# Delta-rule layer: 32-row blocks swapped in every second tile with the solve in three stages, and the gate product as one rounded product over 96 rows

## The reference, cut to what matters

```
def delta_rule(q, k, v, beta):            # per sequence and per head, head size 32
    for each token t:
        pred  = k_t @ S                   # S is a 32x32 state
        delta = beta_t * (v_t - pred)
        S     = S + outer(k_t, delta)
        o_t   = q_t @ S

q = silu(x @ Wq.T); k = silu(x @ Wk.T); v = x @ Wv.T      # 16 heads of 32
beta = 2 * sigmoid(x @ Wbeta.T)
k = k * rsqrt(sum(k*k) + eps)
gate = sigmoid(x @ Wg1.T @ Wg2.T)         # Wg1 is 32x512, Wg2 512x32
og = delta_rule(q, k, v, beta) * gate
out = (og * rsqrt(mean(og*og) + eps)) * g_norm @ Wo.T
```

## Time and profile before

| | us |
|---|---|
| median of 3 runs | 4828.01 |
| lowest and highest | 4825.08, 4836.86 |
| the profiled execution's own time | 4826.68 |
| its span, first to last instruction | 4824.6 |
| PE busy (share) | 4466.7 (93%) |
| DVE busy | 3603.4 (75%) |
| ACT busy | 2416.7 (50%) |
| POOL busy | 707.2 (15%) |

### The profile page before, as it was taken

How to read it: one execution, slowest core, us unless ns; L and a number is a source line. 1 busy time by engine, 2 the same in 40 slices (tenths; PEclk the granted TensorE clock), 3 DMA queues, 4 the chain that set the end, 5 groups by cost and what they waited for, 6 DMA issues and landing times.

```text
span 4824.6 us, 144788 instructions
## 1 busy us (share of the span) xinstructions
PE 4466.7 (93%) x63104; PEld 3089.8 (64%) x63104; DVE 3603.4 (75%) x7890; ACT 2416.7 (50%) x4592; POOL 707.2 (15%) x909
## 2 busy tenths in 40 slices
PE   7999999999999985999999999999999999999998
PEld 6777777777887764565565565565565565565564
DVE  5777767777777773877877877877877877877876
ACT  3344444434444332646646646646646646645645
POOL 0000000000000001122122122122122122122121
PEclk8999999999999997999999999999999999999999
DMA  2223222222322222000000000000000000000000
GB/s 88 56 74 75 73 69 65 65 69 74 78 69 65 65 65 80 1 18 1 19 18 2 19 19 2 19 19 2 19 18 2 19 18 2 19 18 2 19 10 10
DMA packets 352135, 171.76 MB, mean 36 GB/s; under 512 B 300017, under 2 KB 300785, under 8 KB 350737
## 3 DMA queue, kind: packets, MB, share of 16 engines
q1 hardware_dynamic: 342528, 145.20, 11.3%
q10 hardware_dynamic: 8976, 17.30, 1.3%
HBM read 93.74 MB, written 67.63 MB: 33 GB/s over the span
## 4 chain that ended last, share of the span: by engine, by line
PE 45%; DVE 11%; ACT 2%; issue 1%; POOL 1%; DMA 1%; SPq 0%; DVEq 0%; ACTq 0%; POOLq 0%
PE row_psum L1720 10%; PE row_psum L1745 10%; PE row_psum L40 5%; PE row_psum L42 5%; PE row_psum L41 5%; DVE smax L2007 5%; PE row_psum L1733 4%; PE row_psum L1793 1%; DVE xr_lo L1868 1%; PE row_psum L1773 1%; DVE probs L1987 1%; PE row_psum L1507 1%; DVE stats L1834 1%; POOL rstd L1304 1%; PE row_psum L1692 1%
## 5 line engine op out<-in xcount | busy, mean ns | idle before, releaser
L2007 DVE TENSOR_REDUCE smax<-row_psum 128x1 f32<-128x512 f32 x2048 | 1270.5, 681 | 94.8 <-PE row_psum L1720 93.7
L1441 ACT ACTIVATE probs<-row_psum 128x512 f32<-128x512 f32 x2048 | 1090.7, 602 | 350.0 <-PE row_psum L1733 330.5
L1720 PE MATMUL row_psum<-k_stack,q_stack 64*128 64x512 f32 (+1 forms) x2048 | 740.5, 440 | 50.6 <-DVE smax L2007 24.4
L1733 PE MATMUL row_psum<-q_stack,k_stack 64*128 64x512 f32 (+1 forms) x2048 | 733.5, 458 | 20.3 <-ACT probs L1441 8.1
L1720 PEld LDWEIGHTS row_psum<-k_stack,q_stack 64*128 64x128 f32 (+1 forms) x2048 | 354.3, 188 | 499.3 <-DVE smax L2007 367.9
L1745 PE MATMUL row_psum<-probs,v_aug 128*32 128x512 f32 x4096 | 538.9, 603 | 1.7 <-ACT av_sb L1457 0.4
L1733 PEld LDWEIGHTS row_psum<-q_stack,k_stack 64*128 64x128 f32 (+1 forms) x2048 | 319.2, 184 | 223.3 <-ACT probs L1441 155.7
L894 DVE TENSOR_TENSOR lane_t<-lane_t,lane_p 128x30 f32<-128x30 f32 (+14 forms) x960 | 318.3, 332 | 33.0
L40 PE MATMUL row_psum<-wf_hi,xr_hi 128*128 128x320 f32 (+1 forms) x1024 | 332.0, 324 | 5.3 <-DVE xr_lo L1868 3.2
L891 DVE TENSOR_TENSOR lane_p<-lane_t 128x30 f32<-128x30 f32 (+14 forms) x960 | 316.0, 329 | 25.5
L42 PE MATMUL row_psum<-wf_hi,xr_lo 128*128 128x320 f32 (+1 forms) x1024 | 319.0, 312 | 0.0
(11 more groups left out here) (215 smaller groups left out, 9854.2 us busy)
## 6 DMA issues: line engine op xcount, KB each, us to landing
x_sp<-in_x ACTq DMA_DIRECT2D x33, 512.0 KB, 4.3
tri_dram<-tri SPq DMA_DIRECT2D x256, 64.0 KB, 3.2
lane_t<-tri_dram SPq DMA_DIRECT2D x32, 512.0 KB, 3.8
inv_dram<-lane_t SPq DMA_DIRECT2D x32, 512.0 KB, 2.7
inv_b<-inv_dram SPq DMA_DIRECT2D x256, 64.0 KB, 2.3
x_res<-in_x SPq DMA_DIRECT2D x32, 512.0 KB, 3.9
x<-x_res SPq DMA_DIRECT2D x32, 512.0 KB, 3.2
xs<-x SPq DMA_DIRECT2D x16, 1024.0 KB, 5.5
```

Of the source, the lines that this page charges most:

```text
L1441: act.activation(probs[:, h % PROBS, tt, :], ps[:, m % STACK_BANKS, :], ACT.Exp, scale=float(DH) ** -0.5).then_inc(exp_ready, 1)
L1720: pe.matmul(ps[:, bank, :], q_stack[rows, qt, P * st:P * st + P], k_stack[rows, kv, :], start=True, stop=True).then_inc(max_mm, 1)
L1733: pe.matmul(ps[:, m % STACK_BANKS, :], k_stack[rows, kv, P * tt:P * tt + P], q_stack[rows, qt, :], start=True, stop=True).then_inc(score_m ...
L2007: dve.tensor_reduce(smax[:, g, st:st + 1], ps[:, bank_of("max", NT * g + st), :], AX.X, ALU.max).then_inc(max_ready, 1)
```

## The change

**Blocks swapped.** In tile 1 of each span (and only there) the two 32-token blocks of every chunk change places. It is done where x is turned: the four transposes of tile 1 become matmuls with `ident_swapped`. All that follows from x (k, v, beta, the triangles) then has the swapped order in tile 1; `masks_swapped` fits the mask to it. q and gate are put back in token order where ACT takes them out of PSUM: one ACTIVATE for tile 0 and two for tile 1 in place of one for both. `upper` and `product` in tile 1 then read rows 32-63 and 96-127, and `under` reads 0-31 and 64-95.

**Three stages.** The solve becomes `solve_upper`, `solve_product`, `solve_under`, each with 64 matmuls, tile 0 and tile 1 in turn (`both_tiles`), and copies and corrections follow in the order 0, 2, 1, 3 of the groups.

**Gate product.** g1 becomes 96 rows of float32r: rounded, remainder, rounded; Wg2 the same rows as rounded, rounded, remainder. One float32r matmul over 96 rows replaces the float32 matmul over 32. ACT makes the third part (`take_gb`), DVE the second (`split_g1`, behind `correct_queries`).

**Loads at the start.** 4 small DMAs for `ident_swapped`, 12 for `masks_swapped`, 3 in place of 1 for Wg2, all on SP.

```diff
+        def blocks_of(ap, t, h):
+            if t == 0:
+                return ap[:, :, 0:P]
+            return ap[:, :, P:2 * P].rearrange("p g (c h r) -> p g c h r", c=2, h=2)[:, :, :, h, :]
+        def in_token_order():
+            return ((0, None), (0, None)), ((1, 0), (1, 1)), ((1, 1), (1, 0))
 ...
             def take_gb(b, s, first=False):
-                act.activation(g1, BB[0:HD, 0:SPAN], ACT.Copy).then_inc(g1_ready, 1)
+                act.activation(g1[0:HD, :], BB[0:HD, 0:SPAN], ACT.Copy).then_inc(g1_ready, 1)
 ...
+                act.wait_ge(g1_ready, at(b, s, 2, 1))
+                act.activation(g1[2 * HD:3 * HD, :], g1[0:HD, :].bitcast(F32), ACT.Copy).then_inc(g1_ready, 1)
             def take_q(b, s, n):
-                act.activation(kq[:, 2 * n:2 * n + 2, 1 + s, :], (BA, BC)[n][:, :].rearrange("p (g i) -> p g i", g=2),
-                               ACT.Silu).then_inc(q_ready, 1)
+                for place, tokens in in_token_order():
+                    last = act.activation(blocks_of(kq[:, 2 * n:2 * n + 2, 1 + s, :], *tokens),
+                                          blocks_of((BA, BC)[n][:, :].rearrange("p (g i) -> p g i", g=2), *place), ACT.Silu)
+                last.then_inc(q_ready, 1)
 ...
-                            last = pe.transpose((BA, BD)[n][:, SPAN * g + P * t:SPAN * g + P * t + P],
-                                                xn[:, t, P * k:P * k + P], ident[:, :])
+                            if t:
+                                last = pe.matmul(into, xn[:, t, P * k:P * k + P], ident_swapped[:, :], start=True, stop=True)
+                            else:
+                                last = pe.transpose(into, xn[:, t, P * k:P * k + P], ident[:, :])
 ...
+            def block(t, half, late):
+                first = 2 * NB * half + NB * (late if t == 0 else 1 - late)
+                return slice(first, first + NB)
 ...
-            def solve_first(b, s, ahead):
 ...
-                for q in range(2):
+                for n in range(2):
                     if ahead:
-                        pe.wait_ge(tri_ready, at(*ahead, TS * HPT, HPT + q + 1))
-                    for i in range(H):
-                        last = upper(b, s, q, i)
-                    last.then_inc(u0_mm, 1)
+                        pe.wait_ge(tri_ready, at(*ahead, TS * HPT, HPT + n + 3))
+                    both_tiles(upper, b, s, n, u0_mm)
+            def both_tiles(stage, b, s, n, done):
+                for i in range(H):
+                    last = [stage(b, s, 2 * t + n, i) for t in range(TS)]
+                for ins in last:
+                    ins.then_inc(done, 1)
+            def solve_product(b, s):
+                for n in range(2):
+                    pe.wait_ge(u0_ready, at(b, s, 2 * TS, 2 * n + 2))
+                    both_tiles(product, b, s, n, p_mm)
 ...
+            def split_g1(b, s):
+                dve.wait_ge(g1_ready, at(b, s, 2, 1))
+                dve.tensor_tensor(g1[HD:2 * HD, :], BB[0:HD, 0:SPAN], g1[0:HD, :].bitcast(F32), ALU.subtract).then_inc(g1_lo_ready, 1)
 ...
-                correct_lower(*now, 0, behind)
-                correct_lower(*now, 1, behind)
+                for q in IN_TURN:
+                    correct_lower(*now, q, behind)
                 invert_ahead("split")
                 invert_ahead("product")
-                correct_lower(*now, 2, behind)
-                correct_lower(*now, 3, behind)
```

More of the change, by code:

```diff
@@ L180, in _ @@
             sp.dma_start(ident[:, :], ident_in).then_inc(first_in, 16)
+            for pb in range(P // NB):
+                sp.dma_start(ident_swapped[NB * pb:NB * pb + NB, :],
+                             ident_in[NB * (pb ^ 1):NB * (pb ^ 1) + NB, :]).then_inc(first_in, 16)
             sp.dma_start(stage_gb, w_gb).then_inc(second_in, 16)
@@ L325, in take_gate @@
                     act.wait_ge(gate_proj, at(b, s, 2, n + 1))
-                    act.activation(gate[:, s, 2 * n:2 * n + 2, :], (BA, BB)[n][:, :], ACT.Tanh, scale=0.5).then_inc(gate_ready, 1)
+                    for place, tokens in in_token_order():
+                        last = act.activation(blocks_of(gate[:, s, 2 * n:2 * n + 2, :], *tokens),
+                                              blocks_of((BA, BB)[n][:, :].rearrange("p (g i) -> p g i", g=2), *place),
+                                              ACT.Tanh, scale=0.5)
+                    last.then_inc(gate_ready, 1)
             def k_inverse_norms(b, s):
@@ L422, in step @@
                     turned(*further)
-                take_upper(*now, 0)
-                take_upper(*now, 1)
+                for q in IN_TURN:
+                    take_upper(*now, q)
                 if further:
                     take_k(*further, 0)
-                take_upper(*now, 2)
-                take_upper(*now, 3)
-                if further:
                     take_k(*further, 1)
-                for q in range(2 * TS):
+                for q in IN_TURN:
                     take_lower(*now, q)
@@ L578, in upper @@
                 h, half = 8 * n + i // 2, i % 2
-                r = slice(2 * NB * half, 2 * NB * half + NB)
+                r = block(t, half, 0)
                 return pe.matmul(bank[4 + q][r, 2 * HD * (h % 8):2 * HD * (h % 8) + 2 * HD],
@@ L586, in product @@
                 h, half = 8 * n + i // 2, i % 2
[L587 to L589 removed]
+                r = block(t, half, 0)
+                return pe.matmul(bank[4 + q][block(t, half, 1), 2 * HD * (h % 8):2 * HD * (h % 8) + 2 * HD],
+                                 tri[r, s, t, h // HPT, h % HPT, NB * (1 - t):NB * (1 - t) + NB], uw[r, t, h, :], start=True, stop=True)
             def under(b, s, q, i):
@@ L975, in begin @@
                 split_x(*second)
+                split_g1(*second)
                 statistics(*third)
@@ L1005, in step @@
                 correct_queries(*now)
+                if further:
+                    split_g1(*further)
                 invert_ahead("queries")
```

112 lines of the change are left out of this document (58 added, 54 removed).

## The result

The changed kernel takes 4784.6 us (median of 4 runs, 4783.4 to 4800.5), the kernel before 4831.6 us beside it (4 runs, 4825.1 to 4836.9): ratio 0.9913, 95% interval 0.9899 to 0.9927. The forecast was 4789, inside 4762 to 4824. The profiled execution took 4785.5 us with a span of 4783.7.

What follows compares the result with a forecast made beforehand. PE's work was taken as the bound, instruction supply just above its use. Per step -1.35 (solve) -1.24 (gate) +0.49 (ACT) +0.80 (supply) = -1.30 us, over 30 steps -39 us: 4789 us, range 4762 to 4824.

Steps and rivals of the forecast that it cites:

- What bounds the kernel: Whole step: a sum of PE work, PE busy 93% of the span, with instruction supply of 74 per us just above consumption.
- Stages, -1.90 us: Solve: three stages instead of four, each taken as 1.90 us, saving 1.90 us a step.
- The rival with 3.6 us a stage: New solve stages: tiles writing one PSUM bank don't run together, +3.0 us a step, 4917 us; chance 0.05.
- The later first `project_k`, +0.55: Start of the solve: first stage waits for the third triangle's banks, so the first key projection starts 0.55 us later.
- The gate product, -1.24, and +0.65 given back: Chains: two gate products save 0.62 us each; waits for instructions take back 0.65 us a step.
- ACT's pieces, +0.49: Behind the last chain: gate ACTIVATEs split in three per bank add 0.49 us a step on the path, bounds 0 to 1.3.
- DVE's slack, 1.3 us: DVE's gapless stretch after the lanes arrive: 22.5 us, ending 1.3 us before the first state advance is due.
- the DVE rival: DVE's inversion becomes the bound once PE no longer waits for instructions: 4777 us; chance 0.08.
- A wait of L704 for the state: In the chains: PE waiting for DVE's state was named as a sign that the forecast is wrong.
- The start, 0 within -2 and +5: Kernel start: 18 more DMAs on SP, delay nearly covered by room before Wv is needed; 0 us, between -2 and +5.
- The last two steps, 0: Last two steps, without gate or projections: the chain of copies stays as long as before, 0 us.
- nothing given back: Instruction supply takes nothing back, structure alone: -2.10 us in each of 30 steps, 4765 us; chance 0.22.

Runs made afterwards that it cites:

- e5: Changed kernel with the transitions' 128 tiny MATMULs issued twice in every step; some 140 us slower than the changed kernel (145 by medians, 136 by ratios).
- e9: Changed kernel with five extra 512-column float32r MATMULs inside the chains, ahead of the first gate product; 4796.4 us beside 4781.6.
- e2: Kernel before with the rounded 96-row gate product alone, solve and pieces as before; 19 us faster than the kernel before.
- e1: Changed kernel with the gate product put back to four float32 MATMULs of 24 rows; 28 us faster than the kernel before.
- e4: Changed kernel with the gate's tanh in one ACTIVATE per bank, not three pieces; step 54.66 us, gain not shown in the times.
- e10: The changed kernel itself run once more beside later runs on the same chip; 4781.6 us, ratio 0.9900.
- e8: Kernel before with DVE's last two corrections ahead of the inversion in the step without a further span; 3.5 us faster, interval 0 to 10.

## Why the prediction came out right, step by step

- **What bounds the kernel.** Right: PE's own work, with the supply of its instructions close to it. The packets' records, e5 and e9 show the supply; e2 shows what it takes from a gain. The prediction calls 74 per us the most that the queue brings; it was the mean of a stretch in which PE used 69. The shortest distances between packets give 75 to 80, so the number was near, by luck in part.
- **Stages, -1.90 us.** Right: -1.93 in the stretch, 1.92 us a stage. The rival with 3.6 us a stage is out (its own terms sum to +3.4 us a step, not the +3.0 written there, which changes nothing). What the Trainium skill states (TensorEngine Tiling (Array Packing), "Gotcha 1: PSUM Pressure") would have made these stages long. Here two row groups of one tile write one bank, and 128 MATMULs on four row groups take the 1.92 us that 64 on two took before (1.90).
- **The later first `project_k`, +0.55.** The mechanism is right (L953, 17.7 us in 30 steps), the size was low: +0.72 in a step like that of the rows (3.29 to 4.01), +0.90 on the mean. 0.17 us of it I left out: L908's third start is 1.24 us behind the first, and I added 0.62 for its end where the rows of after have the upper start 2.03 us behind the first triangle, not 1.86. The rest are waits for instructions ahead of the uppers and `project_k`, where I had put 0.15 for the whole solve; e1 shows 0.35.
- **The gate product, -1.24, and +0.65 given back.** Right as a sum: -0.56 in the chains against -0.59. e2 gives -0.57 there and +0.7 us of issue waits; the timed runs of e2 are 19 us below before, and with the 4.5 us that its start costs, 23 us or 0.8 a step.
- **ACT's pieces, +0.49.** On the path as said, but half as dear: six L363 take 1.31 us, two L326 took 1.07, +0.24; e4 gives 0.24 too. I had put the six at 1.6. The slope between 512 and 256 columns gave 0.23 for 128 columns with no row to check the overlap of one ACTIVATE with the next.
- **DVE's slack, 1.3 us.** Less was left. The stretch without a gap is 22.6 us (22.5 forecast), 1037.68 to 1060.25, but the state's L982 follows without idle time, because it was due 2.2 us earlier in its step (34.1 us behind the turned blocks, 36.3 in the earlier trace rows) and the lanes came 0.4 later. PE waited for the state 7 times, 2.3 us in all: the DVE rival has begun to bind and costs 0.08 us a step. A wait of L704 for the state was named as a sign of being wrong; it came, but small.
- **The start, 0 within -2 and +5.** The loads of the weights cost nothing that shows, as said. The miss is elsewhere: the new `split_g1` waits 9.72 us at the head of DVE's queue with an inversion behind it. +5.5 us at the third set of turned blocks, +2.3 at the fourth (151.5 before, 153.8 after); the rest was absorbed. I had counted its length, 0.42 us, and not what stands behind its wait.
- **The last two steps, 0.** Wrong: -8.5 us (120.8 to 112.3; -11.3 in e10's trace). The "-12 us in the last two steps" of e1's expectation had step 30 in it. I had moved "the two last L918" in the regular step, where DVE idles, and not in the step without a further span, where they stood behind a DMA and PE waited 4.6 us for them. By e8 this is about half of it; the cause of the rest stays open.

The sum holds partly because misses cancel. Inside a step, the first stage and `project_k` 0 cost 0.43 us more than forecast, and ACT's pieces and the stretch ahead of the chains 0.33 less. From the third set of turned blocks to the first upper of step 31, thirty steps, the gain is 38.7 us (35.3 in e10's trace) for a forecast of 39, the 28 of the table giving 33 of them; 3.2 us of it are step 1 catching up with the late start. Around them +5.5 us at the start and -8.5 at the end (+4.9 and -11.3 in e10) were both put at 0. That these two left a total near the forecast is luck. Without the tail the time would have been 4793 to 4796 us, inside the range and still a gain.

The rival "nothing given back" (4765 us) is shown wrong by e2 and by the packets' records. What the Trainium skill states (Runtime: NRT & Kernel Launch, "Instruction fetch mechanics"), that instruction fetch is hidden, doesn't hold where such small MATMULs run at 90 and more instructions per us (221 transitions with their weight loads in 2.06 us of e5 are over 200 per us): 74 us of waits here, and a kernel 3% slower by 128 more small MATMULs a step (e5 against the changed kernel).

## What to carry to other kernels

Where "issue" waits stand in the middle of a line whose operands are ready, count instructions per us against the packets of the instruction queue: of work taken out of a stretch that runs above that pace about half came back as waits here, and of work put into it 0.7 of 1.18 us was free. Where each packet has a record, look whether the waits end a fixed time behind a landing and stand at one place modulo the packet's number of instructions; that settles it without an experiment. Wide matmuls belong between tiny ones rather than ahead of them. When an instruction is added to an in-order queue, price its wait in each kind of step, the first and last ones too, and not its length alone: here the two largest misses (+5.5 and -8.5 us) had a wait on DVE with an inversion ahead or behind in them.

## What the hardware showed that I had not expected

- A pause ahead of a dense stretch is mostly lost. The same five matmuls cost 30 to 42 us ahead of the first output projection and 15 us (18 by the spans) inside the chains. I had thought of a store that a pause would fill; the count of instructions against packets shows that PE never has more than two packets or so landed and not run.
- A wait for instructions can cost twice. In e5 the granted clock stood at half for 3.5 us behind a wait of 2.3 us that PE spent between tiny matmuls, and wide matmuls paid some 0.9 us a step for it on the mean. In the changed kernel (160 to 1700 us) the clock fell seven times, each time within 2 us of the end of a wait of 1.3 us or more (L570 and L756 behind 1012.22), while ten more waits of over 1 us had no such fall. Waits are not the only way to it: in the kernel before three of six falls have no wait over 0.15 us in the 5 us ahead.
- Three ACTIVATEs of 128, 128 and 256 columns back to back cost 0.12 us more than one of 512 (1.31 against 1.07 us for two banks).
